# Flamingo-style gated layer on one core: last merge block in two 128-row halves, router rows turned by DMA, router products two blocks behind

## The reference, cut to what matters

```python
x = x + tanh(g_xattn[0]) * xattn(_layernorm(x), ctx_1024, w_sim, b_sim, W_qv, b_qv)
x = x + tanh(g_ffn[0]) * ffn(_layernorm(x), w_router, b_router, w1, b1, w2, b2)

# xattn, with e = layernorm(x) (4096 x 512) and q = ctx (3202 x 512)
Sim = (e @ w1)[:, :, None] + (q @ w2)[:, None, :] + einsum('bid,bjd->bij', e * w3, q) + b_sim[0]
hq_hat = softmax(Sim, axis=2) @ q
hc_bar = softmax(max(Sim, axis=2), axis=1) @ e            # one row for all
feats = concatenate([e, hq_hat, e * hq_hat, e * hc_hat]); return feats @ W_qv + b_qv

# ffn: 8 experts, each token to its best 2, 640 places in each expert
gates = softmax(xf @ w_router + b_router); topv, topi = top_k(gates, 2)
pos = cumsum(onehot(topi)) - 1; keep = pos < cap          # tokens beyond 640 are dropped
h = gelu(buf @ w1 + b1); out = h @ w2 + b2                # per expert: 640x512x2048x512
y = sum over the kept experts of w * out / sum of w
```

## Time and profile before

| | |
|---|---|
| median of 3 runs | 2256.39 us (2256.36 to 2259.73) |
| the profiled execution | 2241.02 us |
| its span, first to last instruction | 2239.3 us |
| TensorE busy | 2167.5 us, 97% |
| attention until the first merge product (L363) | to about 1090 us |
| merge and route | about 1090 to 1385 us |
| experts | about 1392 to 2239 us |
| mean granted TensorE clock | 0.99 |

### The profile page before, as it was taken

How to read it: one execution, slowest core, us unless ns; L and a number is a source line. 1 busy time by engine, 2 the same in 40 slices (tenths; PEclk the granted TensorE clock), 3 DMA queues, 4 the chain that set the end, 5 groups by cost and what they waited for, 6 DMA issues and landing times.

```text
span 2239.3 us, 34508 instructions
## 1 busy us (share of the span) xinstructions
PE 2167.5 (97%) x12013; PEld 1122.4 (50%) x12013; DVE 1305.9 (58%) x2667; ACT 1141.5 (51%) x1745; POOL 142.1 (6%) x141
## 2 busy tenths in 40 slices
PE   5999999999999999999999995999999999999997
PEld 2444444444444444444444552656555565647463
DVE  7756566555656655554567875555555464646450
ACT  6765566556556655655433342635445363526260
POOL 0000000000000000000022222010101010010101
PEclk9999999999999999999999997999999999999998
DMA  9534444443444444344988763343333333343401
GB/s 251 130 82 103 107 115 101 107 112 83 99 107 115 100 107 113 77 95 95 273 226 218 205 169 87 133 106 103 99 104 98 108 94 110 91 119 125 129 31 24
DMA packets 484309, 265.89 MB, mean 119 GB/s; under 512 B 423604, under 2 KB 423732, under 8 KB 480172
## 3 DMA queue, kind: packets, MB, share of 16 engines
q1 hardware_dynamic: 473388, 244.90, 41.3%
q0 software_dynamic: 10880, 20.52, 4.8%
HBM read 97.96 MB, written 71.52 MB: 76 GB/s over the span
## 4 chain that ended last, share of the span: by engine, by line
PE 94%; DMA 2%; DVE 1%; ACT 1%; issue 1%; POOL 0%; SPq 0%; POOLq 0%; DVEq 0%; ACTq 0%
PE ps L1213 22%; PE ps L1229 22%; PE ps L1859 19%; PE ps L1874 19%; PE ps L1609 10%; DMA arena<-arena 1%; PE ps L363 1%; PE ps L1619 1%; DMA arena<-in_ctx 1%; DVE arena L738 0%; PE ps L1628 0%; DMA arena<-rows 0%; PE ps L1225 0%; ACT arena L1055 0%; DVE arena L767 0%
## 5 line engine op out<-in xcount | busy, mean ns | idle before, releaser
L1213 PE MATMUL ps<-arena 128*128 128x512 f16 (+1 forms) x2688 | 557.3, 358 | 5.0 <-ACT arena L1034 2.2
L1229 PE MATMUL ps<-arena 128*128 128x512 f16 x2400 | 554.4, 380 | 0.0
L1859 PE MATMUL ps<-arena 128*128 128x320 f16 x3072 | 420.1, 300 | 17.4 <-DMA arena<-rows 17.4
L1874 PE MATMUL ps<-arena 128*128 128x512 f16 x1920 | 415.7, 379 | 0.0
L1213 PEld LDWEIGHTS ps<-arena 128*128 128x128 f16 x2688 | 249.9, 98 | 286.5 <-issue 4.7
L1229 PEld LDWEIGHTS ps<-arena 128*128 128x128 f16 x2400 | 234.1, 98 | 276.7 <-issue 1.9
L1859 PEld LDWEIGHTS ps<-arena 128*128 128x128 f16 x3072 | 301.1, 98 | 136.1 <-issue 17.5
L1034 ACT ACTIVATE arena<-ps,arena 128x512 f32<-128x512 f32 (+1 forms) x224 | 163.6, 732 | 385.9 <-PE ps L1213 385.9
L1874 PEld LDWEIGHTS ps<-arena 128*128 128x128 f16 x1920 | 187.9, 98 | 225.2
L767 DVE SCALAR_TENSOR_TENSOR arena<-arena 128x512 f16<-128x512 f32 x192 | 144.1, 751 | 185.0 <-ACT arena L1055 185.0
L754 DVE TENSOR_REDUCE arena<-arena 128x1 f32<-128x512 f32 (+1 forms) x224 | 139.8, 625 | 192.1 <-ACT arena L1034 191.3
(11 more groups left out here) (229 smaller groups left out, 1366.8 us busy)
## 6 DMA issues: line engine op xcount, KB each, us to landing
arena<-in_L_ffn_w SPq DMA_DIRECT2D x64, 1024.0 KB, 9.2
feats<-arena SPq DMA_DIRECT2D x48, 512.0 KB, 2.8
arena<-in_x SPq DMA_DIRECT2D x32, 512.0 KB, 3.6
rows<-arena SPq DMA_DIRECT2D x13, 774.0 KB, 3.9
out<-arena SPq DMA_DIRECT2D x16, 512.0 KB, 3.0
arena<-in_ctx SPq DMA_DIRECT2D x6, 1024.0 KB, 13.3
arena<-arena SPq DMA_TRANSPOSE x276, 3.1
arena<-in_L_xattn_W_qv SPq DMA_DIRECT2D x4, 1024.0 KB, 8.0
```

Of the source, the lines that this page charges most:

```text
L1213: mm = pe.matmul(out, qT[:, q, s * KD + k, :], ctxT[:, r * KD + k, a:z], start=(k == 0 and s + r == 0), stop=(k == KD - 1 and s == 1))
L1229: mm = pe.matmul(psO[q], turned, ctxN[:, j, r, :], start=(j + s + r == 0), stop=False)
L1859: mm = pe.matmul(psH[:, f % 2, h, :], w1s[:, s, k * F + f * P:k * F + (f + 1) * P], XT[:, r, k, h * HALF:(h + 1) * HALF], start=(k + s + r ...
L1874: mm = pe.matmul(psO[:, t % 2, :], hT[:, f, s, t * P:(t + 1) * P], w2s[:, r, f * D:(f + 1) * D], start=(f + s + r == 0), stop=(f == KF - 1 ...
```

## The change

It has six parts.

1. In the merge, SP turns the normalised rows of a block by two DMAs from SBUF to SBUF, into one of two buffers `xT[v]`. TensorE has no transposes in blocks 1 to 14 but those of block 14 (done in the last body).
2. The router products of block b-2 stand in TensorE's body of block b, after 9 merge products, and the counts of block b-2 after 27 merge products. On VectorE, `route_1(b-2)` and `route_2(b-2)` stand together at the start of the body of block b. The best two are taken from the logits and not from the softmax; the exponentials of the two come along in the same instruction.
3. The last block's two tiles are normalised, turned and routed one after the other, and scattered each for itself, from a third buffer `row[2]`.
4. At the end of the attention, TensorE's pooled product comes after 36 products of the last half unit and not after 12; the fold into the weights comes ahead of the scales, the router's scales after the split of the merge weights.
5. At the start, `norm_weight(0)` and `tail_low` are done before the first unit's low parts of probabilities.
6. In the experts, the rows are turned by two DMAs, one for each half, and layer 1 runs the half as its outer loop: 12 products of one half, then 12 of the other.

```diff
@@ attention, vector @@
         row_max(0, 0, UNIT0)
+        dve.wait_ge(w1_loaded, 32)
+        norm_weight(0)
+        tail_low()
         low(0, 0, 0)
...
-        dve.wait_ge(w1_loaded, 32)
-        norm_weight(0)
         pool_top(0, 0, 0)
-        tail_low()
...
+                if last and i and c == 2:
+                    total_rows()
+                    mg.fold_hc(dve)
+                    for k in range(KD):
+                        mg.fold_part(dve, k)
...
-                    if c == 2:
-                        total_rows()
-                    if c == 3:
-                        mg.scales(dve)
-                        mg.fold_hc(dve)
-                        for k in range(KD):
-                            mg.fold_part(dve, k)
+                if last and i and c == 3:
+                    mg.scales(dve)
@@ attention, tensor @@
-                if last and i and c == 0:
+                if last and i and c == 2:
                     pe.wait_ge(hc_all, 3)
@@ merge_and_route, sync @@
+        def turn_rows(b, v):
+            sp.wait_ge(y_step, YK * (b + 1))
+            apart(sp, sp_passed)
+            for q in range(QT):
+                sp.dma_start_transpose(xT[v][:, q].rearrange("p s k i -> p (s k) i"), halves[v][:, q, 0:2 * D])\
+                    .then_inc(xt_turned[v][q], 16)
...
                 store(2 * n + v, v, n)
-                sp.wait_ge(y_step, YK * (2 * n + v + 1))
-                apart(sp, sp_passed)
+                turn_rows(2 * n + v, v)
                 mg.load_x(sp, x, 2 * n + v + 2, v)
@@ merge_and_route, vector @@
-        def body(b, v, n, routed=2):
+        def body(b, v, n, routed=True, first=False):
             dve.wait_ge(x_loaded[v], 16 * (n + 1))
-            if routed == 2:
-                route_2(b - 2, v, n - 1)
-            y_part(b, v, 0, not routed)
             if routed:
-                route_1(b - 1)
-            y_part(b, v, 1, not routed)
+                route_1_of(b - 2)
+                route_2_of(b - 2, v, n - 1)
+            y_part(b, v, 0, first)
+            y_part(b, v, 1, first)
             norm_part(b, v, n)
...
-        route_2(NB - 2, 0, NB // 2 - 1)
-        route_1(NB - 1)
-        route_2(NB - 1, 1, NB // 2 - 1)
+        dve.wait_ge(x_loaded[1], 16 * (NB // 2))
+        pre_last()
+        route_1_of(NB - 3)
+        route_2_of(NB - 3, 1, NB // 2 - 2)
+        rows_last(0)
+        route_1_of(NB - 2)
+        norm_last(0)
+        lows_last(0)
+        route_2_of(NB - 2, 0, NB // 2 - 1)
+        route_1_last(0)
+        rows_last(1)
+        norm_last(1)
+        lows_last(1)
+        route_2_last(0)
+        route_1_last(1)
+        route_2_last(1)
@@ merge_and_route, vector, the new route_1 to the mask @@
+            s.link(dve.scalar_tensor_tensor(out=lg[:, qs], in0=psG[:, qs], scalar=cR[:, 0:1], in1=bcast(brb, n),
+                                            op0=ALU.mult, op1=ALU.add))
+            apart(dve, dve_passed)
+            for q in range(qs.start, qs.stop):
+                s.step(dve.max(m8[:, q, :], lg[:, q, :]))
+            s.wait()
+            apart(dve, dve_passed)
+            for q in range(qs.start, qs.stop):
+                s.step(dve.max_index(ix[:, q, :], m8[:, q, :], lg[:, q, :]))
+            s.step(dve.tensor_tensor(lgx[:, qs, 0:E], lg[:, qs], spread(m8[:, qs, 0], E), ALU.subtract))
+            s.step(dve.tensor_tensor(lgx[:, qs, E:E + 2], m8[:, qs, 0:2], spread(m8[:, qs, 0], 2), ALU.subtract))
+            s.wait()
+            s.link(dve.tensor_copy(ixf[:, :, qs], ix[:, qs, 0:2].rearrange("p q k -> p k q")))
+            for k in range(2):
+                s.step(dve.tensor_tensor(oh[:, k, qs], bcast(iota8, n), spread(ixf[:, k, qs], E), ALU.is_equal))
+            s.wait()
+            s.step(dve.tensor_tensor(mask[:, qs], oh[:, 0, qs], oh[:, 1, qs], ALU.add))
@@ merge_and_route, tensor @@
         def body(b, v, n, old=True):
             pe.wait_ge(f_loaded[v], 16 * (n + 1))
-            merge(b, v, 0, 0, old)
+            merge(b, v, 0, 0, 3, old)
+            if old:
+                router(v, n - 1)
+            merge(b, v, 0, 3, 9, old)
             if old:
                 counts(b - 2)
-            merge(b, v, 0, 1, old)
+            merge(b, v, 0, 9, FT, old)
...
-            turn_rows(b - 1, 1 - v)
-            merge(b, v, 1, 0, old)
-            router(b - 1)
-            merge(b, v, 1, 1, old)
+            merge(b, v, 1, 0, FT, old)
+
+        def last_body():
+            b = NB - 1
+            pe.wait_ge(f_loaded[1], 16 * (NB // 2))
+            merge(b, 1, 0, 0, 2)
+            router(1, NB // 2 - 2)
+            merge(b, 1, 0, 2, 8)
+            counts(NB - 3)
...
@@ experts, sync @@
-            sp.dma_start_transpose(XT.rearrange("p s k c -> p (s k) c"),
-                                   rows[bass.ds(e * CAP, CAP), 0:D].bitcast(F16)).then_inc(xt_loaded, 16)
+            for h in range(2):
+                sp.dma_start_transpose(XT.rearrange("p s k c -> p (s k) c")[:, :, h * HALF:(h + 1) * HALF],
+                                       rows[bass.ds(e * CAP + h * HALF, HALF), 0:D].bitcast(F16))\
+                    .then_inc(xt_loaded[h], 16)
```

More of the change, by code:

```diff
@@ L1169, in scalar @@
         for k in range(FT):
-            mg.high(act, k, mg.steps)
+            mg.high(act, k, mg.scaled)
             if k == 2:
@@ L1325, in merge_and_route @@
     xn = take([QT, D], F32)
-    row = [take([QT, ROW], F32) for _ in range(2)]
+    row = [take([QT, ROW], F32) for _ in range(3)]
     halves = [r.bitcast(F16) for r in row]
-    xT = take([QT, 2, KD, P], F16)
+    xT = [take([QT, 2, KD, P], F16) for _ in range(2)]
     stats, mv, sd, rs = take([QT, 6], F32), take([QT, 2], F32), take([QT], F32), take([QT], F32)
@@ L1428, in gpsimd @@
         ew.reduce_max(pool, 0)
-        with pool.Fori(NB // 2 - LAST + 1, NB // 2) as n:
+        with pool.Fori(NB // 2 - LAST + 1, NB // 2 - 1) as n:
             send(n)
+        send_block(NB // 2 - 1, 0)
+        for q in range(QT):
+            pool.wait_ge(r_step, RB + RQ * (q + 1))
+            scatter(2, q, 1)
     def vector(dve):
@@ new lines, in pre_last, with rows_last @@
+        def pre_last():
+            s = Steps(dve, y_step, NB - 1, YK + 1)
+            for q in range(QT):
+                s.step(dve.tensor_tensor(x2[1][:, q, :], x2[1][:, q, :], bqb, ALU.add))
+        def rows_last(q):
+            s = Steps(dve, y_step, 0, YK + 1, YB)
+            s.n = 2 + 6 * q
+            s.wait()
+            dve.wait_ge(y_done, QT * (NB - 1) + q + 1)
+            s.link(dve.scalar_tensor_tensor(out=x2[1][:, q, :], in0=psY[1][:, q, :], scalar=cY[:, 0:1],
+                                            in1=x2[1][:, q, :], op0=ALU.mult, op1=ALU.add))
+            s.link(dve.bn_stats(stats[:, q, :], x2[1][:, q, :]))
+            apart(dve, dve_passed)
+            s.step(dve.bn_aggr(mv[:, q, :], stats[:, q, :]))
@@ L1534, in body @@
             norm_part(b, v, n)
-        body(0, 0, 0, routed=0)
+        body(0, 0, 0, routed=False, first=True)
         dve.wait_ge(made, 5)
@@ L1599, in scalar, with merge @@
                     ew.high_part(act, 0, c, False)
-        tail(NB - 1)
+        tail()
     def tensor(pe):
-        def merge(b, v, q, part, old):
-            if old and part == 0:
+        def merge(b, v, q, k0, k1, old=True):
+            if old and k0 == 0:
                 pe.wait_ge(y_step, YK * (b - 2) + 2 * q + 2)
-            for k in range(part * FT // 2, (part + 1) * FT // 2):
+            for k in range(k0, k1):
                 for s, r in ((0, 0), (0, 1), (1, 0)):
@@ L1610, in merge, with turn_tile @@
                                    start=(k + s + r == 0), stop=(k == FT - 1 and s == 1))
-            if part == 1:
+            if k1 == FT:
                 mm.then_inc(y_done, 1)
+        def turn_tile(v, q):
+            for s in range(2):
+                for k in range(KD):
+                    mm = pe.transpose(psR[q][:, s * KD + k, :],
+                                      halves[v][:, q, s * D + k * P:s * D + (k + 1) * P], ident)
+            mm.then_inc(turned, 1)
         def turn_rows(c, v):
```

289 lines of the change are left out of this document (186 added, 103 removed).

## The result

The changed kernel takes 2293.89 us (median of 4 runs, 2293.0 to 2296.89), the kernel before 2256.38 (4 runs, 2252.58 to 2259.73) in the same comparison. The ratio is 1.0179, with a 95% interval of 1.0165 to 1.0193: slower by 1.8%. Forecast were 2290 and a range of 2274 to 2304. The profiled execution took 2294.69 us, its span is 2292.9.

The account below looks back on a forecast made before the run. TensorE, busy 97%, was taken to bound the kernel, and after the change a ring through VectorE's marks; -1.5 + 0.5 + 25.7 + 5 + 4 = +33.7 us on the median 2256.39 gave 2290, range 2274 to 2304.

Parts of the forecast that it names:

- The ring: Steady merge blocks: normalise, mark, count, 45 products close a ring of 17.7 us with a 1.6 us wait; +25.7 us.
- The clock: Merge blocks 7 to 10 and 12 to 14: seven long waits slow the clock, costing 0 to 11 us; 5 taken.
- rival (2): Merge: slow clock follows every long wait, 11 us in place of 5, 2296, or 2306 with short ones; 15 in 100.
- The transfers: Steady merge blocks: turned rows land near S + 15, wanted at S + 19.6, so hidden by 4 us.
- Rival (1): Steady merge blocks: marks are in time and TensorE stays the bound; -12.2 us, 2244, faster than before; 5 in 100.
- The start: Kernel's start and merge's start: -1.5 us for work moved off VectorE's path, +0.5 us by merge block 3.
- the head: Start of the kernel: weight sums and small copy leave VectorE's path ahead of the first full unit; -1.5 us.
- the merge's start: Merge blocks 0 to 3: x load behind two transposes delays block 0's marks; block 3 at 1140.3, term +0.5 us.
- The last block: Last merge block to experts: VectorE's longer list +7.3, row transfer's first half -3.2; term +4 us.
- S: Start of a merge block's first product; forecast in the last block: marks at S + 11.8, last addresses at S + 42.8.
- The base: Whole kernel: the sum +33.7 us against the profiled execution, laid on the median 2256.39, which lies 15.4 higher.

Follow-up runs that it names:

- rows3: prep_moved with the normalised rows and addresses rotating over three buffers in place of two; 2254.43 us, ratio 1.0020.
- fill: The changed kernel with eight idle products more, right ahead of the counts in each steady block; 2282.59 us, ratio 1.0139.
- both: prep_moved with three row buffers and the counts after 33 products in place of 27; 2253.25 us, ratio 1.0014.
- half_turn: both with row-turning DMAs that carry the high halves alone, half the bytes; does not compute the reference's result; 2241.64 us, ratio 0.9951.
- before_rows3: The kernel before with three buffers for the rows and addresses instead of two; 2243.01 us, ratio 0.9954.
- head_rows3: before_rows3 with the attention's edits (weight sums, small copy, pooled product, router's scales moved); 2240.28 us, ratio 0.9942.
- before_again: The kernel before once more, no edit, with a profile of its own; 2251.59 us, ratio 1.0002.
- prep_moved: The changed kernel with VectorE's preparation of expert weights moved behind the next block's routing; 2267.20 us, ratio 1.0068.

## Why the prediction was right, and where it was not

**The ring: right, in mechanism and size, from block 7 on; ahead of it another ring of about the same length held the blocks.** Marks late by 1.6 us, blocks of 17.7: rows3 shows 1.25 and 17.62. In the changed kernel the waits of 1.36, 0.92 and 1.34 us in blocks 4 to 6 look like this ring, but the chain goes through the landing of the scatters there; that the number fits these blocks is luck. With the weight preparation in the ring, 3.8 and 4.3 us were forecast; blocks 7 to 10 waited 3.5 to 3.8, blocks 12 to 14 about 4.05. Taking the preparation out gave back 26.7 us, which includes the slow clock behind these waits. Of the ledger's 46.4, the waits for marks less the saving are 23.6 (32.6 - 9.0), where +25.7 stood.

**The clock: the mechanism right, the size wrong.** The step said that seven long waits cost 0 to 11 us and took 5, "since I have one case of a fall". It was 18.5: a fall behind each of nine waits, the shortest 1.76 us, and 2.1 a wait in place of 1.6. That is rival (2), "every long wait is followed by the slow clock", and fill shows it by taking the idle time away. The Trainium skill ("TensorE: Matmul & The Clock Gate", section "HAM oscillation — how this bites in real kernels") says that a wait in each round lets the next round begin cold. Here the trace agrees for the nine waits of 1.76 us and more in blocks 3 to 14 (0.66 in the 4 us behind one of 3.83) and not for those of 0.92 to 1.36 us, behind which the 54 products keep their 11.81. Other waits of about 2 us show no fall: 1.96 in block 2, and 2.32 in one block of fill. I had weighed the rule at 15 in 100 for having seen a single case.

**The transfers: hidden on average, as forecast, but a chain was missed.** The step counted when the turned rows land and found 4 us of slack; rows were late by 0.3 to 1.8 us in three steady blocks, 2.9 in all. What it did not ask is what more DMA work does to the other DMAs. The features' load takes 9.2 us to landing between 1180 and 1320, by the median, where it took 8.3 before, the scatters land later (5.69 to 6.70 us in the chain), and the high halves wait for the scatters. In the changed kernel itself this is the ring that holds blocks 4 to 7. Rival (1), the marks in time, would not have held even with the marks in time: both has them in time in its steady blocks but for 0.55 and 1.04 us, and late turned rows hold it at 2253. There the prediction's -12 for 14 x 0.89 was too hopeful. It does not appear with half of the turning taken away either: half_turn is 11.9 under the kernel before, but only 1.4 under before_rows3, the kernel before with the third buffer that half_turn has too.

**The start: the head right, the merge's start too small.** Block 3 began 0.5 us later than before, as the net of a gain at the head (1.6, forecast 1.5) and a loss of 2.1 at the merge's start, where +0.5 stood; together +0.5 in place of -1.0. Block 3's first product stands at 1140.34 where 1140.3 was forecast, but that is luck, since the forecast time leaves out the head's gain. The path was another too: VectorE had the marks of block 0 at 1129.64, and what ended last, at 1130.57, was TensorE, which had waited 2.53 and 0.78 us for turned rows and then did 18 products in 5.73 us. The prediction had no slow clock behind this wait. head_rows3 has a gain of 2.7 without that loss.

**The last block: too small.** +4 forecast, +7.2 measured with the experts. The marks of block 13 were ready at S + 11.8 to the tenth (1402.97 - 1391.17); those of block 14 at S + 23.8 and not 21.8, and the last addresses at S + 44.6, not 42.8. TensorE waited 5.90 us at the counts of block 13, and the granted clock was 0.50 in the 4 us behind. From the last addresses to layer 1 the ledger has 4.9 us less than before, and the prediction 5.0 (2.6 for the scatters that go out early, 2.4 for the first half's landing), so this part held. What was missed is 1.8 us on VectorE's list, the 0.8 us still counted for the half-speed clock, and the experts' +0.4.

**The base: a mistake that hid the others.** The difference was summed against the profile (33.7, measured 53.6) and laid on a median that lies 15.4 higher. Both lie near 2290 only because the 20 us that the sum lacked and the 15 that the base had too much nearly cancel, and that is luck. Some 10 of the 15 us are what the scatter ring costs the kernel before in its usual runs: before_again's span is 10.3 us longer than the first profile's, and the third buffer takes 10.5 off. The other 5 are not explained; beside the experiments the median of the kernel before was itself 2251 to 2254. The changed kernel's high halves were held by the scatters for 2.0 us in all. The distance between a profile and the median was a sign of a wait that the profile did not show, and I passed over it.

**Not settled:** the 0.9 us of the ledger without a row, and how the later addresses of the last block (+11.7) divide between VectorE's longer list and the slow clock; no kernel with the last block alone split was run.

## What to carry to other kernels

Before work is moved from the busiest engine to DMAs, count the time of all DMA engines per round as one more engine: here 13 of 17 us were taken, and moving 0.9 us off TensorE cost some 4 there. When an order is fixed on every engine, list each ring that closes through it, the buffers given free by a landing among them; removing one only shows the next. And where the timed runs lie above the profile, look for a wait that is there in some executions only: here one more buffer took 10 us and most of the spread away.

## What the runs showed of the hardware

- A scatter by indirect DMA landed 2.3 to 4.1 us after its issue in the kernel before's first profile (blocks between 1180 and 1320), and 6.1 to 8.8 us four times in its second. The same program does either in different executions; two of the slow ones were issued within 0.8 us of a transposing load of features, where the first profile has the same two 1.6 us ahead of it.
- The clock fell behind each of nine waits of 1.76 us or more in blocks 3 to 14 of the changed kernel's merge and behind none of 0.92 to 1.36; in prep_moved behind 2.08 and not behind 1.70. It did not fall in the 4 us from 1118 around the 1.96 us wait of block 2, nor behind 1.91 in rows3, so these rows give no fixed limit. In fill, eight idle products, 1.89 us, ahead of a wait of 1.75 left the 54 products behind at their full speed (11.81 us), and ahead of 2.32 once so and twice not.
- Transposing DMAs from SBUF to SBUF, 512 KB of rows a block, cost 3.9 to 4.7 us of all 16 DMA engines, an estimate from share times block; half of the bytes took off only 1.9.
